# Attention on one core: ScalarE copies a pair's finished sums of values in two halves instead of at once

## What is computed

```python
h = layernorm(x) * (1 + ca) + sa
q, k, v = h @ wq + bq, h @ wk + bk, h @ wv + bv
attn = einsum('bqhfd,bkhd->bhfqk', q, k) / sqrt(32)
a = einsum('bhfqk,bkhd->bqhfd', softmax(attn), v)
x = x + ga * (a @ wo + bo)
```

## Time and profile before

| | us |
|---|---|
| median of 3 runs | 2801.24 |
| lowest and highest of them | 2797.73 and 2801.27 |
| the profiled execution | 2795.91 |
| its span | 2794.1 |
| granted TensorE clock, mean | 0.995 |

### The profile page before, as it was taken

The page is one execution under the profiler, slowest core; times in us unless marked ns, Lnnn a source line. Parts: engine busy times, 40 slices in busy tenths (PEclk is TensorE's granted clock), DMA queues, the critical chain, the costliest instruction groups (busy, mean ns, idle before and its releaser), DMA issues.

```text
span 2794.1 us, 48987 instructions
## 1 busy us (share of the span) xinstructions
PE 2752.4 (99%) x14654; PEld 1695.8 (61%) x14654; DVE 2181.9 (78%) x2809; ACT 1529.4 (55%) x2959; POOL 1909.4 (68%) x710
## 2 busy tenths in 40 slices
PE   7999999999999999999999999999999999999998
PEld 4788888884444444444444444444444447888887
DVE  4433434348999999999999999999999968676667
ACT  3211111116777676777767777767777764455454
POOL 2433333317999999999999999999999996111110
PEclk9999999999999999999999999999999999999999
DMA  7544443434444334334334334344444443323332
GB/s 268 181 144 137 147 139 132 137 116 137 91 88 100 87 87 100 85 87 100 85 87 100 85 89 98 89 90 93 93 90 91 97 123 114 113 96 108 113 100 81
DMA packets 167645, 307.05 MB, mean 110 GB/s; under 512 B 50001, under 2 KB 91409, under 8 KB 159505
## 3 DMA queue, kind: packets, MB, share of 16 engines
q1 hardware_dynamic: 158496, 240.05, 29.5%
q0 software_dynamic: 9072, 66.06, 11.6%
HBM read 159.12 MB, written 79.82 MB: 86 GB/s over the span
## 4 chain that ended last, share of the span: by engine, by line
PE 74%; DVE 2%; ACT 0%; issue 0%; DVEq 0%; POOL 0%; ACTq 0%; POOLq 0%
PE back_ps L1348 22%; PE back_ps L1362 18%; PE s_ps L1322 17%; PE s_ps L1938 11%; PE back_ps L1379 2%; PE back_ps L1987 2%; PE back_ps L2006 1%; PE back_ps L1959 1%; DVE mx L1237 1%; PE back_ps L1337 0%; PE s_ps L1411 0%; DVE a_lo L1281 0%; ACT h_t L1719 0%; DVE two_sum L1252 0%; DVE xn L1793 0%
## 5 line engine op out<-in xcount | busy, mean ns | idle before, releaser
L1218 ACT ACTIVATE p_t<-back_ps 128x512 f32<-128x512 f32 x2048 | 1114.7, 596 | 432.5 <-PE back_ps L1348 390.7
L1237 DVE TENSOR_REDUCE mx<-s_ps 128x1 f32<-128x1024 f32 x1002 | 1172.4, 1208 | 83.9 <-PE s_ps L1322 76.2
L1128 POOL TENSOR_TENSOR p_sum<-p_sum,p_t 128x2048 f32<-128x2048 f32 x254 | 1166.2, 4591 | 24.8 <-ACT p_t L1218 7.9
L1348 PE MATMUL back_ps<-q_st,k_st 98*128 98x512 f32 x2048 | 809.9, 436 | 3.4 <-POOL ones L1097 2.4
L1348 PEld LDWEIGHTS back_ps<-q_st,k_st 98*128 98x128 f32 x2048 | 343.9, 187 | 592.1 <-ACT p_t L1218 495.7
L1322 PE MATMUL s_ps<-k_st,q_st 96*128 96x512 f32 x2004 | 633.0, 397 | 0.6 <-DVE mx L1237 0.3
L1362 PE MATMUL back_ps<-p_t,v_sb 128*32 128x512 f32 x4096 | 545.8, 605 | 0.0
L1322 PEld LDWEIGHTS s_ps<-k_st,q_st 96*128 96x128 f32 x2004 | 379.0, 189 | 72.5 <-DVE mx L1237 3.2
L574 POOL TENSOR_TENSOR o_lo<-side,o_hi 128x512 fp32r<-128x512 f32 x80 | 104.2, 1303 | 321.4 <-ACT o_hi L544 321.2
L1252 DVE TENSOR_REDUCE two_sum<-p_t 128x512 f32<-128x1024 f32 x256 | 317.8, 1243 | 2.1 <-ACT p_t L1218 2.1
L1128 POOL TENSOR_TENSOR p_sum<-p_t 128x2048 f32<-128x2048 f32 x64 | 312.9, 4889 | 8.6 <-ACT p_t L1218 8.6
(11 more groups left out here) (186 smaller groups left out, 2910.8 us busy)
## 6 DMA issues: line engine op xcount, KB each, us to landing
p_sum<-two_sum POOLq DMA_DIRECT2D x63, 1024.0 KB, 6.9
q_st<-q_hi_d SPq DMA_DIRECT2D x128, 256.0 KB, 4.3
stage<-w_mod SPq DMA_DIRECT2D x48, 512.0 KB, 6.4
q_hi_d<-o_hi SPq DMA_DIRECT2D x64, 256.0 KB, 2.0
q_lo_d<-o_lo SPq DMA_DIRECT2D x64, 256.0 KB, 2.0
q_st<-q_lo_d SPq DMA_DIRECT2D x64, 256.0 KB, 4.1
att_d<-a_sb SPq DMA_DIRECT2D x128, 128.0 KB, 2.3
a_f<-att_d SPq DMA_DIRECT2D x32, 512.0 KB, 4.6
```

Source lines behind the costliest of these rows:

```text
L1128: nc.gpsimd.tensor_tensor(total, before, p_t[:, kt, :, :], ALU.add).then_inc(sum_done, 1)
L1218: nc.scalar.activation(p_t[:, s, c, :], st_ps[:, c % 2, :], ACT.Exp, scale=SCALE)\
L1237: nc.vector.tensor_reduce(mx[:, slot % 2, e:e + 1], s_ps[:, e % 2, :], AX_X, ALU.max)\
L1348: nc.tensor.matmul(st_ps[:, c % 2, :], k_st[:, slot // 2, s * P:(s + 1) * P], q_st[:, slot, jj, h * QW:(h + 1) * QW], start=True, stop=True)\
```

## The change

`take_num` gets a third argument, the half. Each half copies 256 of the 512 columns. The first half carries the waits and stands where the whole copy stood, behind exponential 1 of step 0 (`c == 1`; exponentials are counted from 0 throughout). The second half has no wait of its own, stands behind exponential 2, and raises `num_taken`. Behind the last pair both halves follow each other.

```diff
-        def take_num(pair, par):
-            act.wait_ge(num_done, pair * STEPS + STEPS)
-            if not below(pair, 2):
-
-                act.wait_ge(a_ready, pair - 1)
-            nc.scalar.copy(num_sb[:, par, :], num_ps[:, :]).then_inc(num_taken, 1)
+        def take_num(pair, par, half):
+            cols = slice(half * QW // 2, (half + 1) * QW // 2)
+            if half == 0:
+                act.wait_ge(num_done, pair * STEPS + STEPS)
+                if not below(pair, 2):
+
+                    act.wait_ge(a_ready, pair - 1)
+            part = nc.scalar.copy(num_sb[:, par, cols], num_ps[:, cols])
+            if half == 1:
+                part.then_inc(num_taken, 1)
...
-                    if c == 1 and s == 0 and not below(pair, 1):
-                        take_num(pair - 1, 1 - par)
+                    if c in (1, 2) and s == 0 and not below(pair, 1):
+                        take_num(pair - 1, 1 - par, c - 1)
...
-        take_num(NPAIR - 1, (NPAIR - 1) % 2)
+        for half in range(2):
+            take_num(NPAIR - 1, (NPAIR - 1) % 2, half)
```

## The result

The changed kernel takes 2810.36 us (median of 6 runs, 2806.8 to 2811.09), the kernel before on the same chip 2798.48 us (median of 6, 2796.61 to 2801.27). The ratio is **1.0038**, with a 95% interval of 1.0026 to 1.0051: the change makes the kernel slower, by 11 us by the ratio and by 11.9 by the two medians. The profiled execution is the median one, 2810.36 us with a span of 2808.5.

What follows compares the result with a forecast made beforehand. The prediction took TensorE to be the bound, with ScalarE's lateness passing into step 0. 16.1 us lost, less 7.5 and 0.1 regained, gave +8.5: 2801.24 + 8.5 = 2809.7 us, range 2801 to 2815.

Steps and rivals of the forecast that it cites:

- How long step 0 is: Step 0 of every pair was to take 3.36 us, from 3.26 or 3.19, against 3.10 for a plain step.
- both kinds: Pairs whose copy begins 0.14 us into step 0 (short kind, step 3.19) or 0.21 (long kind, 3.26).
- The first half: Behind exponential 1, holding ScalarE 0.27 us: exponential 2 and tile 0's load back on time, worth 7.5 us.
- the cover: Margin between the first half's end (0.48 us in the long kind) and exponential 2's start (0.54): 0.06 us.
- The second half: Behind exponential 2, it delays exponential 3 by 0.26 us; tile 1's load moves from 1.67 to 1.93.
- 62 x 0.26 = 16.1: Loss in us from the second half: 0.26 in step 0 of each of 62 pairs.
- What was put at nothing: Edits given no cost: num_taken's later increment (0.4 us cover), GpSimd's division, DMAs, SP and GpSimd queues, step 1's exponentials 0 and 1.
- all of it lands in TensorE: Tile 1's load in step 0 was to pass the whole 0.26 us lateness on to the step's length.
- A: Rival: the wait for tile 1 is no bound, step 0 is 3.10, 7.6 us won, 2793.6 us; 7%.
- B: Rival: part of the lateness is swallowed behind tile 1; if half, +0.5 us, 2801.7 us; 12%.
- C: Rival: a half copy costs ScalarE 0.33 to 0.35 us; +13.5 us, 2814.7 us; 10%.
- the prediction's sum by that rule: With the Trainium skill's 0.306 us hold for a half on ScalarE, the total was given as 62 x 0.30 - 7.6 = +11.0.

## Why the prediction was right

**The forecast held in direction and nearly in size**: +8.5 us (a ratio of 1.0030), measured 1.0038 with 1.0026 to 1.0051; the median of 2810.36 lies inside 2801 to 2815, 0.7 us from the 2809.7 forecast. That closeness is luck: the kernel before had a median of 2798.48 this time and not 2801.24, and from there the forecast would be 2807.0. The change measured between the medians is 11.9 where 8.5 was forecast.

- *How long step 0 is*: 3.36 was forecast, alike in both kinds; measured 3.37 and 3.37.
- *The first half*: exponential 2 at 0.54, the load for tile 0 at 1.19, both as forecast. The half's hold was put at 0.27; it is 0.25 (1398.92 to 1399.17), so the cover in the long kind was a little wider than the 0.06 counted.
- *The second half*: exponential 3 was to begin at 1.29 and began at 1.28, the load for tile 1 at 1.93 and came at 1.95. The rest sits behind the exponential's start: from there to tile 1's load it is 0.67 (1399.17 to 1399.84), in a plain step 0.64. The exponential itself accounts for it: behind a copy it is drawn with 0.617, behind another exponential with 0.592, and the load follows its end by 0.05 in both. The term 62 x 0.26 = 16.1 should have been 62 x 0.27 = 16.7, which makes the sum 9.1, and the step 0s gave 9.3.
- *What was put at nothing*: the prediction let no DMA and no queue move and counted nothing behind the last pair but the two halves. The step 0s made 9.3 us; behind the last load of the scores 3.3 more appeared, with 2.1 given back in the 63rd pair.
- *That all of it lands in TensorE*: shown with a half and with a whole copy behind exponential 2, both passed on whole. Rivals A and B are refuted, and so is C, whose half would have held ScalarE 0.34.
- *What the ScalarE page of the Trainium skill (ScalarE: Activation LUTs, What ACT_TABLE_LOAD costs) gave*, 0.306 for a half, was too high: two halves end to end take 0.65, so the second begins 0.28 behind the first, and 0.25 is all that an exponential waits behind one. (With 0.306, and not 0.30, the prediction's sum by that rule is +11.4, not +11.0.)
- *The error*, in a rival and not in the forecast: A was priced at the full 7.6 us for a loss-free step 0. The prediction had read GpSimd's 1003 of 1040 us as room and looked no further. It counted busy time only; the round also has the 0.67 us in which GpSimd waits for its own last sum, which is idle time, and which has the same mean of 0.67 in all six traces in which it was read. With it a round is 25.99 of TensorE's 26.03. Step 0 free of loss was worth 0.9996 when measured, 0.9973 only with GpSimd relieved.

## What to carry to other kernels

Cutting an instruction in two helped here only where each part stood in a gap of its engine; between two instructions that run end to end, with an engine waiting for the second, even a half arrived whole at the other side. So find, for each place in the list, how late the next instruction may be, and not only how long the inserted one is: behind exponential 3 the same half cost step 0 nothing. And before you price a gain, take every other engine's round from one instruction to the same one a round later, with its own waits on itself in it, not its busy share.

## What the runs showed of the hardware

A product of two SBUF tensors on VectorE, 128 x 512, took 2.31 us in the mean while GpSimd was adding nearly all the time; in `finish`, where GpSimd has little to do, VectorE's product of 128 x 1024 has a median of 1.23. By the Trainium skill (SBUF — State Buffer, SBUF: two separate sides) a VectorE instruction with both inputs in SBUF and a GpSimd instruction that reads SBUF exclude each other, and the one that comes second waits until the first is done. The trace agrees: 62 of the 64 products begin during a GpSimd instruction and end 0.55 to 0.56 us behind its end, whatever their own length (up to 3.73); the two that met none took 0.68 and 0.69. VectorE's reductions from PSUM run beside the same additions at 1.21 us.

An instruction of ScalarE holds the engine for less than it is drawn: 0.25 of 0.37 us for the copy of 256 columns (0.28 where another copy follows), 0.48 of 0.59 for 512, 0.49 of 0.60 for the exponential. Where instructions follow closely, count from start to start.
